# Routed convolutions on one core: emptying PSUM, adding residuals and fetching experts in another order in the last two phases

## The reference

```
x = x + L0(gn(x))      # gn: group norm of 32 groups of 2 channels
x = x + L1(gn(x))

L0(x): three times
    attn   = softmax over the pixels of (x Wk) q, two heads
    logits = pooled (attn, x Wv) Wmlp;  weights = masked softmax(logits / 1.5)
    wsel   = the two largest of four weights, scaled to sum 1
    x_mod  = x * (1 + attn_map * 1024 * softplus(alpha))
    x      = sum over experts e of wsel[e] * (conv3x3(x_mod, We[e]) + be[e])
L1(x): r = relu(batch norm(x Wr)); w = r Ws + bs       # 16 groups x 9 taps a pixel
    out = sum over 9 taps of w * (3x3 neighbours of (x Wi + bi))
```

## Time and profile before

| what | value |
|---|---|
| median of 3 timed runs | 675.14 us (674.09 to 675.57) |
| the profiled execution | 673.33 us, of it span of the trace 671.5 us |
| PE busy | 628.5 us, 94% of the span |
| DVE busy | 522.5 us, 78% |
| ACT, POOL busy | 326.7 us, 49%; 181.0 us, 27% |
| granted TensorE clock, mean | 0.985 of full speed |

### The profile page before, as it was taken

The page is one execution under the profiler, slowest core; times in us unless marked ns, Lnnn a source line. Parts: engine busy times, 40 slices in busy tenths (PEclk is TensorE's granted clock), DMA queues, the critical chain, the costliest instruction groups (busy, mean ns, idle before and its releaser), DMA issues. The chain is left out here.

```text
span 671.5 us, 15413 instructions
## 1 busy us (share of the span) xinstructions
PE 628.5 (94%) x5984; PEld 250.0 (37%) x5984; DVE 522.5 (78%) x816; ACT 326.7 (49%) x451; POOL 181.0 (27%) x193
## 2 busy tenths in 40 slices
PE   6868999889999999999999989798999999999995
PEld 7523333323333333333333323233444444444442
DVE  5699875997766666766688676969898898888885
ACT  3754632311422242133315545743687787788761
POOL 2100330007300810280047000531344234235231
PEclk9979899999999999999999979999999999999998
DMA  8930030042433253125422416000122222132132
GB/s 323 220 66 1 1 84 1 1 95 71 98 93 73 72 139 101 50 71 141 95 67 55 116 31 149 1 9 9 25 57 48 48 64 48 41 70 49 40 72 63
DMA packets 67461, 47.95 MB, mean 71 GB/s; under 512 B 53602, under 2 KB 54596, under 8 KB 67396
## 3 DMA queue, kind: packets, MB, share of 16 engines
q1 hardware_dynamic: 67108, 46.82, 28.3%
q10 hardware_dynamic: 288, 0.21, 0.1%
HBM read 35.15 MB, written 9.76 MB: 67 GB/s over the span
## 5 line engine op out<-in xcount | busy, mean ns | idle before, releaser
L759 PE MATMUL conv<-xpad,comb 64*64 64x512 f32 x2016 | 228.1, 597 | 4.3 <-DVE x L1386 4.2
L1646 DVE TENSOR_TENSOR x<-conv,x 128x512 f32<-128x512 f32 x288 | 177.9, 683 | 24.0 <-PE conv L814 22.7
L759 PEld LDWEIGHTS conv<-xpad,comb 64*64 64x64 f32 x2016 | 75.4, 134 | 136.6 <-issue 121.7
L814 PE MATMUL conv<-rstack,wse 98*128 98x512 f32 x288 | 95.9, 434 | 2.9 <-DVE xin L1432 0.9
L830 PE MATMUL att<-x,cmp 64*32 64x512 f32 x1280 | 79.7, 596 | 0.0
L814 PEld LDWEIGHTS conv<-rstack,wse 98*128 98x128 f32 x288 | 48.1, 188 | 72.3 <-DVE x L1646 65.7
L1318 DVE SCALAR_TENSOR_TENSOR xpad<-att,x 128x1024 f32<-128x1024 f32 x46 | 54.1, 1219 | 25.7 <-PE att L609 25.3
L960 ACT ACTIVATE x<-conv,bias 128x512 f32<-128x512 f32 x40 | 25.2, 682 | 90.5 <-PE conv L759 90.5
L728 PE MATMUL conv<-row_sums,comb 64*64 64x512 f32 x480 | 58.5, 617 | 9.0 <-DVE xin L1432 7.7
L1798 POOL TENSOR_TENSOR x<-x,xin 128x1024 f32<-128x1024 f32 x15 | 35.9, 2393 | 111.5 <-ACT x L1112 111.5
L951 ACT ACTIVATE comb<-experts,small 128x768 f32<-128x768 f32 (+1 forms) x33 | 27.4, 859 | 78.1 <-PE conv L728 31.9
(11 more groups left out here) (212 smaller groups left out, 749.8 us busy)
## 6 DMA issues: line engine op xcount, KB each, us to landing
experts<-forms SPq DMA_DIRECT2D x72, 192.0 KB, 4.0
experts<-forms SPq DMA_DIRECT2D x72, 144.0 KB, 2.8
x<-in_x SPq DMA_DIRECT2D x32, 256.0 KB, 5.6
out<-comb SPq DMA_DIRECT2D x30, 256.0 KB, 3.2
rstack<-rstack SPq DMA_DIRECT2D x16, 128.0 KB, 2.3
experts<-in_We SPq DMA_DIRECT2D x1, 1152.0 KB
forms<-experts SPq DMA_DIRECT2D x2, 576.0 KB, 5.7
out<-comb SPq DMA_DIRECT2D x4, 128.0 KB, 2.2
```

The source lines that it names most:

```text
L759: last = nc.tensor.matmul(conv[own[to], h, HW * rows:HW * rows + HW], comb[own[rows], q % 2, n, tap(t)], xpad[own[rows], 2 * (q % 2) + n, ...
L814: nc.tensor.matmul(conv[:, unit, cols], wse[:, ORDER[i], :], rstk[s][0:RR, cols], start=True, stop=True).then_inc(exp_full, 1)
L1646: v.tensor_tensor(img(prod[i])[:, rows, :], img(conv[:, unit, :])[:, rows, :], xip[s][:, kh + 16 * h:kh + 16 * h + 16, kw:kw + W], ALU.mul ...
```

## The change

Four pieces of program order move; no instruction is added or taken away.

```diff
# SP
-            for q in range(GATHER_FROM, QP * LAST + 6):
+            for q in range(GATHER_FROM, QUADS - 1):
                 gather(q)
             eng.wait_ge(residual_added, residuals(QP * LAST + 2))
             for dst, src in LATE_CONSTS:
                 eng.dma_start(dst, src).then_inc(late_consts_in, 16)
-            for q in range(QP * LAST + 6, QUADS):
-                gather(q)
+            gather(QUADS - 1)
# DVE
                         final(q - 1, 1)
                     if j == 3 and attended:
                         reduce_attention(p + 1, 0)
+                    if q - 1 in SHORT_FINAL:
+                        add_residual(q - 1)
                     if q + 1 < QUADS:
...
+                        if q >= QP * LAST and q not in SHORT and j == 3:
+                            final(q, 0)
                         modulate(q + 1)
                         if q in SHORT:
                             finish_rows(q, 0)
+                        elif q >= QP * LAST and j < 3:
+                            final(q, 0)
                         if q + 1 in SHORT:
                             sum_rows(q + 1)
                             subtract_rows(q + 1)
-                    if q >= QP * LAST and q not in SHORT:
+                    if q == QUADS - 1:
                         final(q, 0)
-                    if q - 1 in SHORT_FINAL:
-                        add_residual(q - 1)
-                    if q == QUADS - 1:
                         final_stats(q - 1)
```

## The result

The changed kernel takes 664.66 us (median of 4 runs, 663.91 to 664.74), the kernel before 675.12 us beside it (4 runs, 674.09 to 675.57): ratio 0.9845, 95% interval 0.9828 to 0.9862. The profiled execution after took 664.74 us, its span 663.0.

A forecast was written before the change was run, and what follows sets the result against it. PE, the busiest engine, was held by waits for `final`, 7.7 us in all. Terms 5.30 + 3.76 - 2.8 - 1.7 - 0.65 gave 3.9 us off the 675.14 median: 671.2 us, range 666.2 to 673.5.

The forecast's parts named there:

- Quad 20, +5.30: At quad 20's first stage, emptying quad 19's first half before the modulation removes PE's 3.94 us wait and low clock: 5.30 us gained.
- Quad 22's two waits, +3.76: Before quad 22's first and second stages, both PE waits of 1.88 us go as work comes earlier: 3.76 us gained.
- The collision, -2.8: At quad 22, both long POOL passes fall among DVE's four row passes, so PE waits 2.8 us before the second stage.
- The clock, -1.7: Behind PE's forecast 2.8 us wait at quad 22, the granted clock falls, costing 1.7 us.
- The residual of 22, -0.65: After the second finish, DVE's residual of quad 22 holds POOL's product behind the inverse root, delaying PE's projection: 0.65 us lost.
- Rival (a): At quad 22, POOL misses the row passes, so no wait or clock loss there: gain 8.4 us, time 666.7, chance 0.20.
- What the fetch is worth: Quad 22's fetch, no longer behind constants and register loads on SP, starts at 390.1 instead of 400.54 and is fully hidden.
- The base: The gain, summed in the profiled execution's time of 673.33 us, was subtracted from the timed runs' median, 675.14.

## Why the prediction was wrong

- *Quad 20, +5.30:* right, 5.32 measured. The new wait was 1.16 where 1.32 was forecast, the clock stayed at 1.00, and DVE's wait for the map kept the 1.4 us that were left as cover (1.39).
- *Quad 22's two waits, +3.76:* right in kind, 4.21 measured. Each stop of PE costs some 0.2 us beside its wait, as groups without one overlap by that (quad 21 ends at 401.82 + 12.20 = 414.02, quad 22 starts at 413.84).
- *The collision, -2.8: here the prediction failed.* The step was "So both POOL passes, 2.6 us each as DVE felt them, fall among the four row passes, as the first is there before the third row pass starts." Being there before the third pass gave POOL one turn, not two: its first pass held the differences by 2.3 us, its second, ready at 412.76, went behind the second difference pass and was through at 418.00. With one turn `final(21, 1)` is in time, and PE's wait is 0 instead of 2.8. In the traces without a pause POOL had to come before the *second* row pass to get both turns, and here it missed that by 0.07 us. The mechanism exists at the forecast size (2.57 for 2.8), shown without the fetch edit, taken away again by a later POOL and brought about in the changed kernel by a pause; the forecast of where it begins was wrong by one pass. Why POOL's second pass got no turn between the difference passes stays open: a pause there gives it one, but the missing gap alone, as the run with the fetch alone shows, doesn't keep POOL out.
- *The clock, -1.7:* not paid, as there was no wait. Behind such a wait it is 1.5 us or nothing from one execution to the next.
- *The residual of 22, -0.65:* right, 0.50. The inverse root kept its 1.67 us and only the product behind it was held (0.70 for 0.20). The Trainium skill's "SBUF — State Buffer", section "SBUF: two separate sides", by which the first one has the ports for the whole instruction, fits the long passes again (2.3 to 2.7 us each) and not the root: by the page the term would have been -2.2. Which of two waiting passes goes next isn't told by the starts of their rows: POOL's second, of 412.76, went behind DVE's of 413.73.
- *Rival (a)* has the right gain (8.4, against 8.5 between the spans) for a wrong reason: POOL did not miss the row passes, it got one turn among them instead of two. That the gain agrees is luck.
- *What the fetch is worth* was told wrongly, though it didn't enter the sum: the early fetch was put down to SP's new order, and the early residual of quad 18 brings it without that (390.72). Either of the two moves alone does.
- *The base.* 4.6 us of the miss of 6.5 are the terms above, with the 0.34 at the start and the -0.87 at the end of the table. The other 1.9 are the execution that was profiled before: its 673.33 us lay 1.8 below its median, that of the changed kernel at its median. On the chip of the later runs, where the medians are 674.13 and 664.79, the gain is 9.3.

What is open: what decides between POOL and DVE when both have a pass ready, why the outcome hangs on some hundredths of a microsecond and yet was the same in both traces of the changed kernel, and whether the 668.72 is the other one.

## What to carry to other kernels

Where passes of two engines don't run together, don't only count those that overlap: write down in which order they come, which of them wait for one before them, and what each turn would cost; if the order hangs on less than the spread of your estimates, forecast both outcomes. A wait that makes the order fixed (POOL after the differences) costs nothing here and is safer than an order that happens to fall well. And before crediting an edit with an early transfer, follow the semaphore that its queue waits on: one early instruction on another engine had moved the queue already.

## What was not expected of the hardware

- POOL 0.07 us behind a DVE pass or 0.12 before it went with 4.0 us in the medians, through one turn more or less. In all three traces in which POOL came before the second row pass of quad 22 (by 0.12 and 0.40 without the fetch edit: 408.60 against 409.00 in the repeat; by 0.85 with late residuals: 412.03 against 412.88) it got two turns among the row passes; in the three in which it came behind that and before the last row pass, and DVE made no pause (the changed kernel twice, the fetch alone), it got one.
- PE's clock fell to 0.51 at 448.30 behind a wait of 0.87 us, in a stretch where DVE is nearly always busy, while waits of 1.16 and 1.88 in dense work left it at 1.00.
